# Spreading the step between attention and layer 2 over the edge network's blocks, and standing the softmax's steps one to two tiles later, in a four-layer graph network on one core

## The reference, cut to what matters

```python
h = relu(layernorm(x))                                     # layer 0: relational graph attention, 4 heads
e = leaky_relu(el + er)                                    # one score per edge and head
ex = exp(e - segment_max(e, dst)[dst])
denom = segment_sum(ex, dst)
x = x + segment_sum((ex / denom[dst]) * feat[src], dst) + h_bias
h = relu(layernorm(x))                                     # layer 1: GCN over clusters
logits = D^-1/2 (A + I) D^-1/2 (h + sum(cluster)) @ W + bias        # deg from the edges
x = x + h + softmax(logits) @ cluster
h = relu(layernorm(x))                                     # layer 2: message passing with an edge network
e = relu(edge_attr @ ee_w1 + ee_b1) @ ee_w2 + ee_b2
h = 2h + segment_sum(h[src] + e, dst)                      # then a 3-layer MLP, layernorm, relu
...                                                        # layer 3: layernorm, mean of neighbours, two products
```

## Time and profile before

| | us |
|---|---|
| time before, median of 3 runs | 3806.15 (3799.23 to 3808.66) |
| profiled execution, its own time | 3784.75 |
| its span in the profile | 3782.8 |
| attention, 25 batches | 476.2 to 1257.2 |
| the step | 1257.6 to 1410.7 |
| edge network, 125 blocks | 1410.7 to 2108.5 |
| busy over the span | PE 84%, DVE 53%, ACT 33%, POOL 26% |

### The profile page before, as it was taken

How to read it: one execution, slowest core, us unless ns; L and a number is a source line. 1 busy time by engine, 2 the same in 40 slices (tenths; PEclk the granted TensorE clock), 3 DMA queues, 4 the chain that set the end, 5 groups by cost and what they waited for, 6 DMA issues and landing times.

```text
span 3782.8 us, 51083 instructions
## 1 busy us (share of the span) xinstructions
PE 3168.3 (84%) x15984; PEld 1976.4 (52%) x15984; DVE 1988.3 (53%) x5773; ACT 1237.2 (33%) x3508; POOL 992.0 (26%) x1015
## 2 busy tenths in 40 slices
PE   2999368888888557877778879998999999999998
PEld 2544135555555246766678334444555555555545
DVE  6666457777777453543334235333555555551334
ACT  1222256666666223322223113000444444430000
POOL 0000556666664526766661000000000000000000
PEclk6899678898899659899989969999999999999999
DMA  4455334444442001111112744333000000013232
GB/s 110 129 171 172 119 111 142 137 135 136 136 135 61 1 7 23 25 23 23 23 23 29 253 135 122 103 102 115 6 6 4 5 4 6 6 57 90 70 103 80
DMA packets 232496, 296.61 MB, mean 78 GB/s; under 512 B 120614, under 2 KB 156891, under 8 KB 228187
## 3 DMA queue, kind: packets, MB, share of 16 engines
q1 hardware_dynamic: 187995, 195.19, 17.6%
q0 software_dynamic: 39968, 66.75, 6.8%
q10 hardware_dynamic: 4320, 31.95, 2.1%
HBM read 220.38 MB, written 73.40 MB: 78 GB/s over the span
## 4 chain that ended last, share of the span: by engine, by line
PE 61%; DVE 13%; issue 10%; ACT 6%; DMA 3%; DVEq 3%; another core or an unknown queue 2%; SPq 0%; ACTq 0%
PE PS L1044 14%; PE PS L912 13%; PE PS L898 7%; PE PS L885 6%; PE PS L737 5%; PE PS L786 4%; PE PS L855 4%; ACT BG L568 4%; DMA BG<-a_d 2%; PE PS L853 2%; DVE BG L1498 2%; DVEq L1429 2%; DVE SUMS L1413 1%; ACT SL L651 1%
## 5 line engine op out<-in xcount | busy, mean ns | idle before, releaser
L494 POOL DMA_INDIRECT a_d<-VAL,IDXS x499 | 496.5, 995 | 331.8 <-issue 114.8
L462 POOL DMA_INDIRECT BG<-feat_d,IDXST x500 | 484.1, 968 | 283.6 <-PE PS L737 135.2
L1044 PE MATMUL PS<-BG,SL 128*128 128x512 f32 (+1 forms) x1440 | 539.1, 530 | 12.1 <-ACT SL L651 12.1
L568 ACT ACTIVATE BG<-BG,SL 128x64 f32<-128x64 f32 x2000 | 485.3, 334 | 29.8 <-issue 29.8
L898 PE MATMUL PS<-OHB,AL 128*128 128x128 f32 x2000 | 314.2, 294 | 126.3 <-issue 113.9
L1044 PEld LDWEIGHTS PS<-BG,SL 128*128 128x128 f32 x1440 | 277.0, 195 | 251.8 <-issue 222.4
L1455 DVE TENSOR_TENSOR SUMS<-SUMS,PS 128x256 f32 x500 | 210.4, 421 | 370.3 <-PE PS L898 239.1
L855 PE MATMUL PS<-OHB,BG 128*128 128x128 f32 x2000 | 392.0, 323 | 0.0
L898 PEld LDWEIGHTS PS<-OHB,AL 128*128 128x128 f32 x2000 | 292.7, 207 | 162.7 <-issue 142.2
L499 POOL MEMSET BG<- 128x7680 f32 x1 | 6.5, 6498 | 1378.7 <-DVE MV L1666 1378.7
L1413 DVE TENSOR_TENSOR SUMS<-SUMS,PS 128x384 f32 x500 | 276.4, 553 | 161.3 <-PE PS L737 98.6
(11 more groups left out here) (273 smaller groups left out, 4291.3 us busy)
## 6 DMA issues: line engine op xcount, KB each, us to landing
BG<-a_d SPq DMA_DIRECT2D x171, 256.0 KB, 4.2
AL<-a_d SPq DMA_DIRECT2D x137, 256.0 KB, 2.6
a_d<-SUMS SPq DMA_DIRECT2D x30, 1088.0 KB
feat_d<-SUMS ACTq DMA_DIRECT2D x30, 1040.0 KB, 5.0
BG<-rel_d SPq DMA_DIRECT2D x100, 160.0 KB, 3.2
BG<-in_edge_attr_dram SPq DMA_DIRECT2D x124, 128.0 KB
SUMS<-a_d SPq DMA_DIRECT2D x52, 256.0 KB, 2.6
BG<-feat_d,IDXST POOLq DMA_INDIRECT x500
```

What stands on the lines that cost most here:

```text
L462: pool.indirect_dma_start(RING[:, t // NB % 3, t % NB, :], None, table, bass.IndirectOffsetOnAxis(ap=IDXST[:, t:t + 1], axis=0),).then_inc ...
L494: pool.indirect_dma_start(a_d.rearrange("n (w o) -> (n w) o", o=1), bass.IndirectOffsetOnAxis(ap=IDXS[:, t:t + 1], axis=0), VAL[:, t:t + 1 ...
L568: last = act.activation(v, v, ACT.Copy, scale=EXT[:, b % 2, k, 1 + q:2 + q])
L1044: last = pe.matmul(PS[:, to + q, 0:width], lhs[:, i, c, :], w[:, c, q * width:(q + 1) * width], start=(c == 0), stop=(c == kc - 1))
```

## The change

- The step's work is cut up. After the block's four tiles, PE and DVE take: in block 0 PE the weight sums (30 turns), in block 1 DVE their inverses, in blocks 3, 5, ... 61 the attention's output for one node tile each (SUM_V), in block 63 the means, in block 66 the layer norm's scale (SCALE_V), in blocks 69 to 98 one row tile each: norm on ACT, turn and logits on PE, copy and addition on DVE (NORM_V), in block 99 the rest.
- HS is set to zero in two parts: DVE columns 0 to 1023 before block 0, ACT the other 2856 after block 0's relu; DVE waits for it (`hs_zero`) before block 1.
- The degrees' broadcast (8 products and 8 copies) stands behind the edge network.
- The first two `net_turn` and the two `hidden` of block 0 stand in the last attention batch; edge loads begin there too. Edge turns use one PSUM bank instead of two, and stand behind a block's second tile; `hidden` stands behind tiles 0 and 2 instead of 1 and 3.
- Scatters: the 60 of the step go to the edge network too. 459 follow its tiles, one each, of which the k-th waits for tile k.
- The other one-hots stand in every second block from 4 to 50.
- Softmax: DVE at tiles 0, 4, 7, 10; PE at 4, 7, 10, 16; ACT at 14.

```diff
-                elif t < BESIDE_GAT + 2 * NT:
-                    pool.wait_ge(s("f0_done"), 1 + (t - BESIDE_GAT) // 2)
                 else:
-                    pool.wait_ge(s("agg_ps"), 20 + T + t - BESIDE_GAT - 2 * NT)
+                    pool.wait_ge(s("agg_ps"), 20 + T + t - BESIDE_GAT)
...
-                    if b + 1 < NS and k == 13:
+                    if b + 1 < NS and k == 14:
                         soft_exp(b + 1)
...
-            SOFT_PE = {2: soft_turn, 5: soft_ends, 8: soft_carry, 15: soft_back}
+            SOFT_PE = {4: soft_turn, 7: soft_ends, 10: soft_carry, 16: soft_back}
...
-            SOFT_DVE = {0: soft_in, 3: soft_local, 6: soft_rows, 9: soft_shift}
+            SOFT_DVE = {0: soft_in, 4: soft_local, 7: soft_rows, 10: soft_shift}
...
+                if v == 0:
+                    act.wait_ge(s("dve_mark"), DVE_MARKS["adj_ready"])
+                    act.wait_ge(s("a_zero"), 16 * NT)
+                    act.activation(HS[:, :, FIRST_SUMS:AW], bc(EPSC[:, 0:1].unsqueeze(1), [P, 2, AW - FIRST_SUMS]),
+                                   ACT.Copy, scale=0.0).then_inc(s("hs_zero"), 1)
...
             for v in range(NE):
                 for k in range(4):
                     hidden_sum(v, k)
-                    if k == 0 and v + 2 < NE:
+                    if k == 1 and v + 2 < NE:
                         net_turn(v + 2)
-                    if k % 2 == 1 and v + 1 < NE:
+                    if k % 2 == 0 and v + 1 < NE:
                         hidden(v + 1, k // 2)
+                if v == 0:
+                    weight_sums()
+                for t in range(NT):
+                    if v == SUM_V(t):
+                        sums_turn(t)
+                    if v == NORM_V(t) + 1 and t < EARLY:
+                        row_logits(t)
+                    if v == NORM_V(t):
+                        row_turn(t)
...
+                    for t in range(NT + 1):
+                        if v == SUM_V(t):
+                            if t < NT:
+                                attention_out(t)
+                            if t >= 1:
+                                last = attention_stats(t - 1)
+                    if v == STATS_V:
+                        step(last)
+                        row_means()
...
+                    if 0 <= v - NORM_V(0) < NT:
+                        row_logits_in(v - NORM_V(0))
+                    if v == NORM_V(NT):
+                        logits_out()
```

More of the change, by code:

```diff
@@ L514, in norm_row @@
                                bias=NBI[:, t:t + 1]).then_inc(s(f"n{l}_hr"), 1)
[L516 to L524, removed]
+            rstd(0)
+            for t in range(NT):
+                if t >= 10:
+                    act.wait_ge(s("n0_tp"), t - 9)
+                norm_row(0, t)
             act.wait_ge(s("small_in"), 16 * 15)
@@ L571, in _ @@
                         soft_take(b + 1)
[L573 to L579, removed]
             def edge_turned(v):
@@ L915, in adjacent @@
                 last.then_inc(s("a_used"), 1)
-            pe.wait_ge(s("added"), T + 10)
-            for t in range(NT):
-                last = turn(PS[:, 2, (H + 1) * t:(H + 1) * (t + 1)], SUMS[0:H + 1, 0, t * P:(t + 1) * P], H + 1)
-            last.then_inc(s("pe_mark"), 1)
+            SOFT_PE = {4: soft_turn, 7: soft_ends, 10: soft_carry, 16: soft_back}
+            for b in range(NS):
+                for k in range(NB):
+                    if b + 1 < NS and k in SOFT_PE:
+                        SOFT_PE[k](b + 1)
+                    gat_sum(b, k)
+                    if b == NS - 1 and k == 11:
+                        net_turn(0)
+                    if b == NS - 1 and k == 15:
+                        net_turn(1)
+                    if b == NS - 1 and k in (16, 18):
+                        pe.wait_ge(s("dve_mark"), DVE_MARKS["edge_start"])
+                        hidden(0, (k - 16) // 2)
@@ new lines, in weight_sums, with sums_turn @@
+            def weight_sums():
+                pe.wait_ge(s("added"), T + 10)
+                for t in range(NT):
+                    last = turn(PS_DEN[:, (H + 1) * t:(H + 1) * (t + 1)], SUMS[0:H + 1, 0, t * P:(t + 1) * P], H + 1)
+                last.then_inc(s("pe_mark"), 1)
+            def sums_turn(t):
+                if t == 0:
+                    pe.wait_ge(s("dve_mark"), DVE_MARKS["dg_in"])
+                else:
+                    pe.wait_ge(s("f0_done"), t)
+                for c in range(2):
+                    last = turn(PS_ROW1[:, c * P:(c + 1) * P], SUMS[:, c + 1, t * P:(t + 1) * P], P)
+                last.then_inc(s("f0_tp"), 1)
@@ new lines, in row_turn, with row_logits @@
+            def row_turn(t):
+                pe.wait_ge(s("n1_hr"), t + 1)
+                if t >= 1:
+                    pe.wait_ge(s("n1_ht"), t)
+                for c in range(2):
+                    last = turn(PS_ROW1[:, c * P:(c + 1) * P], ring(t)[:, c * P:(c + 1) * P], P)
+                last.then_inc(s("n1_tp"), 1)
+            def row_logits(t):
+                pe.wait_ge(s("n1_ht"), t + 1)
+                for c in range(2):
+                    last = pe.matmul(PS_LOGIT[t // EARLY][:, t % EARLY * K:(t % EARLY + 1) * K], HT1[:, HT1_AT(t), c, :], GW[:, c, :],
+                                     start=(c == 0), stop=(c == 1))
+                last.then_inc(s("n1_mm"), 1)
@@ L1448, in edge_adds @@
                         edge_one_hot(v + 1)
-                    if 20 <= v < 20 + 6 * LB:
-                        first_one_hot((v - 20) // 6, (v - 20) % 6)
+                    for i in range(6 * LB):
+                        if v == FIRST_V(i):
+                            first_one_hot(i // 6, i % 6)
+                    if v == 1:
+                        dve.wait_ge(s("hs_zero"), 1)
                     for k in range(4):
```

204 lines of the change are left out of this document (113 added, 91 removed).

## The result

The changed kernel takes **3688.95 us** (median of 4 runs, 3683.93 to 3698.28). Beside it the kernel before took 3807.40 us (3799.23 to 3813.83). The ratio is 0.9696 (95% interval 0.9679 to 0.9712), so 118 us are gone where 163 were forecast (3643 us, range 3590 to 3706).

What follows compares the result with a forecast made beforehand. Hand-overs bound the step, scatters the edge network, PE and DVE waits the attention. From 3806 us, -159 + 28 + 8 + 6 + 2 + 7 - 55 = -163 gave 3643 us, range 3590 to 3706.

Steps and rivals of the forecast that it cites:

- The ceiling: Edge network: scatters, not PE, set the pace, at about 1.4 to 1.5 us per scatter, holding up everything else.
- +28: Edge network: 60 scatters moved in from the step each turn a 1.01 us tile into 1.48 us, +28 us.
- node and row work (+8): Edge network blocks: node and row tiles fit under the scatters' pace, +8 us, taken between 0 and 66.
- the 7.0 us rival: Edge network: 30 node tiles cost 7.0 us each in line, row tiles 5.0; slower than before, 3995 us, chance 4%.
- the start's 6: Start of the edge network: zeroing on DVE and filling on ACT delay the first blocks, +6 us.
- The step: Between attention and edge network: its chain of hand-overs leaves the path whole, -159 us.
- The softmax: Attention batches: PE does two more tiles before its first softmax turn, 2.3 us a batch, -55 us.
- the softmax's move gives nothing: Rival, attention: PE's stall moves from the softmax's turn to the four-tile lead; -108 us, 3698 us, chance 20%.
- The end: Behind the last edge addition: degree products stand alone, partly at the full clock, +7 us.
- wait of 19.75 us: Behind the last scatter: the wait for edge attributes comes again, later, at the same price, net 0.
- The rule of the shared ports: Edge network: 30 additions of a row to X, 12.5 us, would hold scatters up; sum -151 us, 3655 us.

## Why the prediction was right, and where it was wrong

*The ceiling* was read right. It was taken from two paces that stand side by side in one trace, and it carried +28 (+26 measured alone), the near-zero price of node and row work (+8), and the refusal of the 7.0 us rival. The edge network grew by 43 us where 28, 8 and a part of the start's 6 were forecast. On one chip, the network is 727 and 729 us in the two kernels with the step spread over it and 717 in the one with the 60 scatters alone, so node work, row work and the start cost 10 to 12 us. One block was not priced: block 99, with the rest of the logits, takes 11.38 us in after and 5.60 in before. That blocks 3 to 98 and 99 to 114 are alike (6.02 and 6.11 us) was named as its test, and the last scatter stood 46 us before the last addition, where about 40 was forecast. The refused rival took 7.0 us for each of 30 node tiles; the first 12 in the same trace take 1.09 us beside dense scatters. What the prediction could not see is that the ceiling is a matter of the chip: on the third chip scatters slow no block, so neither the 28 us nor the shelter for node and row work exists there.

*The step* left 155 us, seam and start together, of 153 forecast.

*The softmax* is the failed step: "I take 2.3 us a batch ... x 24 = -55 us". The rival "the softmax's move gives nothing" described what happened, "PE's stall only changes its name", at 3698 us, and 3688.95 is nearer to it than to 3643. The two additional tiles are real work, but DVE's first addition of a batch comes when it came before, and PE may be only four tiles ahead of it: what PE does early it waits for later. The 4.0 us that DVE waits in a batch were taken for a reserve that PE's earlier tiles could fill; the idle time of PE, 4.7 us a batch before, was 4.6 after, and DVE's ahead of its additions 5.1 in both. The reading of the rows was low as well: 2.6 and 4.0 us a batch count only the waits whose release the trace names, and all of them are 3.2 us for the first turn and 5.1 for the additions.

*The end* cost 14 us where 7 were forecast: 3.5 of the difference are the degree products, which ran partly at half clock (10.2 us). The other 3.5 are within what the end differs from trace to trace of the same code (1673 to 1679 us in the kernels with the old step, 1680 to 1692 in the others on such chips). The load's "wait of 19.75 us", taken at the same price again, was a wait of 10.02 in before and 5.82 in after, so 4 us of luck in a term of net 0.

*The rule of the shared ports* would have held scatters up by the 30 additions of a row to X. The rule shows in single scatters: in before, of the 75 that start beside a VectorE instruction with two inputs in SBUF 56 last over 1.0 us, of the other 424 none. It shows one way only: of the 125 one-hots of the network in after 81 start while a scatter runs, and they last 683 ns, the others 688. The 12 us stayed away because in after only 9 scatters start beside an addition of a row to X, and one of them lasts over 1.0 us. The mean scatter is 990 ns in after and 995 before.

*The total*: -155 + 11 + 43 + 14 is -87 between the traces, -118 between medians, and the fault of 55 us in one term lay inside the range only because the rival with that term at zero was in it. The step and the scatters were understood; the softmax's term, a third of the forecast, was not, and there the range held by the breadth of its bounds.

## What to carry to other kernels

A wait moved away from an engine gains time only if the engine that ends the stage starts sooner; where a lead of a fixed number of tiles ties two engines, compare the sum of idle time before and after, not the wait that was aimed at. Two paces of the same loop in one trace, with and without a side stream, show a ceiling and what can be hidden under it for next to nothing. Test such a ceiling by thinning the side stream in the second half of one run, since a comparison between chips can mix it with the chip's own pace.

## What the runs showed of the hardware

- On three of the four chips of the experiments, where GpSimd issues one indirect scatter per 1.5 us, releases reach the other engines late again and again: PE has 46 gaps of 0.9 to 6.5 us in 685 us, 2.3 on average. At one scatter per 2.2 us there is no such gap (0 in 273 us).
- Behind a pause the hold-up doesn't start with the first scatter: 12 node tiles beside ten scatters took 1.09 us each, the following ones up to 7.0.
- It doesn't hang on the elements: 128, 64 or 16 in a scatter give blocks of 5.9 to 6.2 us.
- On one chip it doesn't occur at one scatter per 1.31 us, and the same program takes 3465 instead of 3781 to 3808 us there. Why chips differ no run shows, nor what the recording has to do with it.
- Beside the gaps PE loses about as much again while it is busy: the network takes 734 us in after and 525 on the chip without gaps, 209 us more, of which the gaps over 0.9 us are 115; the granted clock is 0.88 (1275 to 1960 us) against 1.00 (1280 to 1560).
- GpSimd issues a scatter of 128 elements every 1.26 us at best (0.96 busy and 0.30 between) and every 1.31 on average on the chip without gaps, where the last one landed 19.4 us after its issue.
